# A nine-tap convolution moved from TensorE and VectorE to ScalarE products summed by accumulating transfers

## Chip, cores, metric

One core of one Trainium2 chip. The metric is the device time of one execution in microseconds (us). The kernel before takes 526.42 us, the median of three runs from 525.8 to 526.88 us.

## What is computed

Four sequences (chunks) of 512 tokens by 128 channels pass a gated convolution block and a mixture of 160 experts, each with a modulated layer norm and a residual. Cut to what matters:

```python
h = layernorm(x) * (1 + ca) + sa                 # modulation per chunk
h = rmsnorm(h) @ in_w.T + in_b                   # 128 -> 512
gate, val = sigmoid(h[..., :256]), h[..., 256:]
a = (dwconv4(val) @ A) @ Bm                      # four taps, rank 16
b = silu(dwconv9(val) + sym_b)                   # nine taps, per channel
y = concat([a @ ha.T, (b @ pw.T) @ hb.T]) @ fuse.T
x = x + ga * (h_attn_in + (gate * y) @ out_w.T + out_b)
h = layernorm(x) * (1 + cb) + sb
probs = sigmoid(h @ router_w.T)                  # top 8 of 160, normalized, times 2.5
x = x + gb * (sum_e combine_e * (silu(h @ w_gate_e.T) @ w_down_e.T) + shared(h))
```

`h_attn_in` is the modulated input, the block's own residual. The nine-tap branch is `b`: each channel of `val` is multiplied by nine weights at shifts of -4 to 4 tokens, and the products are added.

## The kernel before

Channels lie on the 128 partitions and the 512 tokens of a chunk along the free axis. The 256 channels of `val` are two halves, q = 0 and q = 1. Matmuls that need float32 accuracy are three float16 ones (`split`, L1159 to L1164: high by high, low by high, high by low).

**Experts.** Four experts make a duo; a chunk has 40 duos (`DUOS`), the kernel 160. For duo J, TensorE multiplies up (`up`, six matmuls), ScalarE applies silu out of PSUM (L803, two halves) and rounds the product with the combine weights to float16 (L822), VectorE multiplies by those weights (L1133, for the first two duos L1129 out of PSUM) and takes the rounding's rest (L1122), and TensorE multiplies down for duo J-4 (six matmuls, `LAG` = 4). SP loads the combine weights of a duo, broadcast, from a small HBM array (`c_all<-combine`), three duos ahead into a ring of four (`CRING`).

**Attention part.** It is cut into named items for a chunk. `walk` calls them in one written order, and every engine runs through that order for itself, doing its own share of each item: first the prologue (chunk 0 and part of chunk 1, setup, the first splits of the expert weights into high and low float16), then 160 times a duo followed by the items that the table `WITH` names for it. So an engine's queue is that order, filtered, and waits are on semaphores only. Items of chunk c+1 and c+2 are spread between the duos of chunk c.

**The nine taps before** come in two forms. For (chunk, half) in `BYDVE`, that is (0,1), (2,0), (2,1), (3,0), (3,1), TensorE makes `val` in a PSUM bank (`val0`, `val1`) and VectorE adds nine scaled shifts (`tapq:i`, L1030 and L1036). The bias part is an image `symb`, made by one matmul and copied by ScalarE (`setup(6)`, item `symb`). For (0,0), (1,0) and (1,1), TensorE does all: the input projection and each tap folded into one weight matrix (`wc_h`, `wc_l`), three matmuls for a tap, 27 for a half (`convq:i0:i1`), plus one for the bias. The folded weights of a half take a broadcast load, a multiplication (L866), a rounding (L630) and a subtraction (L870), for both halves.

**Residual.** `base0` (L1009) multiplies the modulated input by the output gain; `base1` adds it (L1012) and the gained bias (L1015) to `res` on VectorE; `x2` (L1064) adds the attention output. `ha` (L1002) adds the shift of the modulation, on VectorE.

**GpSimd** (POOL) does memsets, small copies and twelve tiny powers for norms (`rstd` L610, `rms` L613, `rstd2` L616). It issues no transfer.

**Order around the first duo.** The prologue holds chunk 0 whole, with its router (`max`, `swap`, `cw`, `sum`), the combine weights (`cT`, `c0`, `c1`), `conv` of chunk 1 up to tap 7, and seven splits of expert weights (`split_hi` on ScalarE L687, `split_lo` on VectorE L955); the other 13 follow in chunk 0's duos. Duo 0's product (L1129) needs `c0`; duo 2's needs the combine weights stored to HBM (`c_out`) and loaded again.

## Time and profile before

| | before |
|---|---|
| median of three runs | 526.42 us |
| profiled execution: span from first to last instruction | 523.2 us (the profile gives no other time for it; the median lies 3.2 us above) |
| TensorE busy | 510.4 us, 98% |
| VectorE busy | 492.7 us, 94% |
| ScalarE busy | 421.3 us, 81% |
| GpSimd busy | 27.6 us, 5% |
| mean granted TensorE clock | 0.997 |
| share of 16 transfer engines, the SP queue | 60.2% |

A busy time counts an instruction to its end, and the ends of one instruction and the start of the next overlap. How often an engine can start an instruction is read from the starts in the timeline. A shape such as 128x512 is partitions by elements.

### The profile page before, as it was taken

Reading aid. Unit: us, or ns where it says so; the run is one execution under the profiler, and the core shown is the slowest. Engines: PE = TensorE matmul, PEld = TensorE weight load, DVE = VectorE, ACT = ScalarE, POOL = GpSimd, SP = SyncE. Lnnn points to the kernel's source line nnn. Section 1 sums busy time; section 2 is a strip of 40 time slices with the busy share of each in tenths; the row PEclk is TensorE's granted clock in tenths of the full one; section 3 lists DMA queues with packets and bytes.
Section 4 is the critical chain, followed back from the end, with each engine's and each line's share of the span. In section 5 each row is a group of like instructions: output and inputs, shape, how many; then the busy total and the mean of one; then the engine's idle time right before and its main releaser. Section 6 shows DMA issues by size and latency. Waiting matters only on the chain.

```text
span 523.2 us, 7224 instructions
## 1 busy us (share of the span) xinstructions
PE 510.4 (98%) x2441; PEld 245.8 (47%) x2441; DVE 492.7 (94%) x630; ACT 421.3 (81%) x686; POOL 27.6 (5%) x45
## 2 busy tenths in 40 slices
PE   7989999999999999999999999999999999999996
PEld 5644544445454444444554444444553444444442
DVE  5999999999999999999999999999899799999995
ACT  5488899988999877787799877876799877777774
POOL 5100200004100000000100000000100000000000
PEclk9999999999999999999999999999999999999999
DMA  8897566645364666655455766665463676666650
GB/s 265 301 369 290 179 207 209 199 157 162 122 203 143 237 186 199 200 202 172 162 161 146 232 189 202 202 209 163 134 196 114 219 240 206 206 202 205 201 177 21
DMA packets 33309, 101.88 MB, mean 195 GB/s; under 512 B 3700, under 2 KB 8952, under 8 KB 33272
## 3 DMA queue, kind: packets, MB, share of 16 engines
q1 hardware_dynamic: 33272, 101.43, 60.2%
q8 instruction: 19, 0.31, 0.2%
q14 instruction: 18, 0.15, 0.1%
HBM read 98.52 MB, written 2.36 MB: 193 GB/s over the span
## 4 chain that ended last, share of the span: by engine, by line
PE 69%; DVE 19%; issue 5%; ACT 2%; DMA 2%; POOL 1%; SPq 1%; DVEq 0%; ACTq 0%
PE bank L1162 22%; PE bank L1164 21%; PE bank L1163 21%; DVE g_all L1122 7%; DVE s_all L1133 4%; DVE w L955 2%; PE bank L1309 2%; DMA res<-x_dram 2%; POOL rms L613 1%; PE bank L1319 1%; PE bank L1408 0%; DVE st L965 0%; DVE key L1099 0%; DVE s_all L1129 0%; ACT g_all L822 0%
## 5 line engine op out<-in xcount | busy, mean ns | idle before, releaser
L803 ACT ACTIVATE s_all<-bank 128x512 f32<-128x512 f32 x320 | 189.4, 594 | 69.4 <-PE bank L1164 68.5
L1122 DVE TENSOR_TENSOR g_all<-s_all,g_all 128x1024 f16<-128x1024 f32 x160 | 195.8, 1224 | 13.0 <-ACT g_all L822 12.7
L1133 DVE TENSOR_TENSOR s_all<-s_all,c_all 128x1024 f32<-128x1024 f32 x158 | 193.2, 1223 | 2.4 <-DMA c_all<-combine 2.4
L822 ACT ACTIVATE g_all<-s_all 128x1024 f16<-128x1024 f32 x160 | 168.2, 1052 | 2.1 <-DVE s_all L1133 1.9
L1162 PE MATMUL bank<-x_h,w 128*128 128x512 f16 x320 | 121.3, 379 | 1.0 <-ACT s_all L803 1.0
L1162 PE MATMUL bank<-g_all,w 128*128 128x512 f16 x320 | 121.3, 379 | 0.8 <-DVE g_all L1122 0.7
L1163 PE MATMUL bank<-g_all,w 128*128 128x512 f16 x320 | 121.3, 379 | 0.0
L1164 PE MATMUL bank<-g_all,w 128*128 128x512 f16 x320 | 121.3, 379 | 0.0
L1164 PE MATMUL bank<-x_l,w 128*128 128x512 f16 x320 | 121.3, 379 | 0.0
L1163 PE MATMUL bank<-x_h,w 128*128 128x512 f16 x320 | 121.3, 379 | 0.0
L1162 PEld LDWEIGHTS bank<-g_all,w 128*128 128x128 f16 x320 | 31.3, 98 | 41.0 <-DVE g_all L1122 3.6
L1162 PEld LDWEIGHTS bank<-x_h,w 128*128 128x128 f16 x320 | 31.3, 98 | 40.7 <-ACT s_all L803 4.6
L1163 PEld LDWEIGHTS bank<-g_all,w 128*128 128x128 f16 x320 | 31.3, 98 | 37.8 <-issue 1.3
L1164 PEld LDWEIGHTS bank<-g_all,w 128*128 128x128 f16 x320 | 31.3, 98 | 37.8
L1164 PEld LDWEIGHTS bank<-x_l,w 128*128 128x128 f16 x320 | 31.3, 98 | 37.8
L1163 PEld LDWEIGHTS bank<-x_h,w 128*128 128x128 f16 x320 | 31.3, 98 | 36.0 <-issue 1.3
L1036 DVE SCALAR_TENSOR_TENSOR attw<-bank,vec,attw 128x511 f32<-128x511 f32 (+3 forms) x40 | 29.9, 747 | 0.3
L955 DVE SCALAR_TENSOR_TENSOR w<-w 128x1024 f16<-128x1024 f32 x20 | 24.4, 1226 | 0.2 <-ACT w L687 0.2
L687 ACT ACTIVATE w<-w 128x1024 f16<-128x1024 f32 x20 | 20.8, 1054 | 0.6 <-DVE w L955 0.4
L613 POOL TENSOR_TENSOR rms<-mse,mhalf 128x4 f32<-128x4 f32 x4 | 9.5, 2378 | 197.8 <-DVE mse L977 197.8
L1309 PE MATMUL bank<-attw,wb 128*128 128x512 f32 x32 | 14.7, 592 | 0.0
L616 POOL TENSOR_TENSOR rstd<-ve,mhalf 128x4 f32<-128x4 f32 x4 | 6.7, 1685 | 136.2 <-DVE ve L1077 136.2
(236 smaller groups left out, 376.8 us busy)
## 6 DMA issues: line engine op xcount, KB each, us to landing
c_all<-combine SPq DMA_DIRECT2D x158, 512.0 KB, 4.5
w<-w_dram SPq DMA_DIRECT2D x20, 512.0 KB, 10.1
combine<-cT SPq DMA_DIRECT2D x4, 256.0 KB, 3.1
out_dram<-res SPq DMA_DIRECT2D x3, 256.0 KB, 3.0
s_all<-mats_dram SPq DMA_DIRECT2D x1, 640.0 KB, 6.7
attw<-symT_dram SPq DMA_DIRECT2D x1, 576.0 KB, 8.0
c_all<-symT_dram SPq DMA_DIRECT2D x1, 576.0 KB, 6.6
mod<-rows_mod SPq DMA_DIRECT2D x1, 576.0 KB, 4.4
```

The lines of the kernel that those rows point to most:

```text
L613: g.tensor_tensor(rms[:], mse[:], mhalf[:, 0:NT], ALU.pow).then_inc(s["rms_set"], 1)
L687: a(high(i), staged(i), ACT.Copy, scale=ES).then_inc(s["w_hi"], 1)
L803: a(sr[J % SRING][:, q * L:(q + 1) * L], U[q][:], ACT.Silu, scale=1.0 / ES).then_inc(s["s_done"], 1)
L822: a(gh[n % GRING], sr[n % SRING], ACT.Copy).then_inc(s["hi_set"], 1)
L955: e.scalar_tensor_tensor(out=low(i), in0=staged(i), scalar=ES, in1=high(i), op0=ALU.mult, op1=ALU.subtract).then_inc(s["w_lo"], 1)
L1036: e.scalar_tensor_tensor(out=acc[:, t0:t9], in0=val[:, t0 + d:t9 + d], scalar=v("sym_k", mid + d), in1=acc[:, t0:t9], op0=ALU.mult, op1=AL ...
L1122: e.tensor_tensor(gl[n % GRING], sr[n % SRING], gh[n % GRING], ALU.subtract).then_inc(s["lo_set"], 1)
L1133: e.tensor_tensor(sr[J % SRING], sr[J % SRING], cr[J % CRING], ALU.mult).then_inc(s["gm"], 1)
L1162: mm(dst, lh, rh, start=start, stop=False)
L1163: mm(dst, ll, rh, start=False, stop=False)
L1164: return mm(dst, lh, rl, start=False, stop=stop)
L1309: last = mm((A1, A2)[q][:], wb[:, i, q * P:(q + 1) * P], s32[:, i, :], start=False, stop=(i == ML - 1))
```

## The change

- `BYACT`: the nine taps of chunks 1, 2 and 3, both halves, are now items `mulq:i`. ScalarE computes tap i as `scale * val + bias` from the PSUM bank, `scale` the tap's weight and `bias` that weight times the projection's bias; the middle tap goes straight to the accumulator `s32`, the other eight alternately to one of two buffers for a half (`part`). GpSimd issues for each of the eight a transfer that adds the buffer to `s32` in SBUF; it waits for the product and for the transfer before on that half. ScalarE waits before tap i > 2 until the transfer of tap i-2 has landed, as it reuses that buffer.
- (0,0) stays with TensorE, (0,1) with VectorE. The folded weights exist for half 0 only, and `symb` for half 1 of chunk 0 only: a broadcast load, L866, L630, L870 and the image for the other half go.
- `base1` of chunks 1 to 3 is two adding transfers from GpSimd, `ha` of chunks 2 and 3 one each.
- The order is new throughout. Items `ss`, `cT`, `c0`, `c1`, `cT_sb` of chunk 0 come after duo 0 instead of before it; three more splits come after it.

```diff
-BYDVE = ((0, 1), (2, 0), (2, 1), (3, 0), (3, 1))
+BYPE = ((0, 0),)
+BYDVE = ((0, 1),)
+BYACT = ((1, 0), (1, 1), (2, 0), (2, 1), (3, 0), (3, 1))
...
-        18: ((2, "ha"),),
-        19: ((1, "ya0"), (11, "split_lo"), (12, "split_hi"),),
...
+        18: ((1, "mul0:8"), (11, "split_lo"), (1, "gate"),),
+        19: ((1, "mul1:8"),),
...
+        4: ((3, "nb"), (2, "mul1:2"), (2, "zl"), (2, "base0"), (2, "mul0:3"), (2, "mul0:4"), (2, "zh"),
+            (2, "mul1:3"),),
+        5: ((2, "gate"),),
+        6: ((2, "mul1:4"), (3, "t1b"),),
...
+        15: ((3, "ha"), (2, "mul0:7"),),
+        16: ((2, "mul1:7"),),
+        18: ((2, "zmv"), (2, "mul0:8"), (2, "mul1:8"), (2, "base1"),),
+        20: ((2, "tanh0"), (3, "rms"), (3, "square"),),
+        21: ((2, "wo"),),
+        22: ((2, "silu0"),),
...
+def shifts(i):
+
+    d = (0, 1, -1, 2, -2, 3, -3, 4, -4)[i]
+    return d, max(0, -d), L - max(0, d)
...
-        wc_h, wc_l = sb("wc_h", [P, KS * DI], F16), sb("wc_l", [P, KS * DI], F16)
+        pbuf = sb("pbuf", [P, 2 * L + KS * P])
+        kb = sb("kb", [P, ML * KS])
...
+        def part(q, i):
+
+            at = (1 - q) * 2 * L + i % 2 * L
+            return pbuf[:, at:at + L]
...
-            sp.dma_start(pool_d[:, 2048:2048 + KS * P], symT[:, KS * P:].broadcast_to([P, KS * P])).then_inc(s["ld_sym1"], 16)
...
+                elif n[0:3] == "mul" and n[5] != "0":
+                    q, i = int(n[3]), int(n[5])
+                    d, t0, t9 = shifts(i)
+                    turns = rounds(c, q)
+                    pool.wait_ge(s[f"mul{q}"], turns * KS + i + 1)
+                    if i > 1:
+                        pool.wait_ge(s[f"add{q}"], 16 * (turns * (KS - 1) + i - 1))
+                    g.dma_start(s32[:, q, t0:t9], part(q, i)[:, t0:t9], accum_op=ALU.add).then_inc(s[f"add{q}"], 16)
+                elif n == "ha" and c > 1:
+                    pool.wait_ge(s["h_set"], c + 1)
+                    g.dma_start(h[:], modr(c, 0), accum_op=ALU.add).then_inc(s["ha_dma"], 16)
+                elif n == "base1" and c:
+                    tiles = slice(c * NT, c * NT + NT)
+                    pool.wait_ge(s["u_set"], c + 1)
+                    g.dma_start(res[:, tiles, :], t1[:], accum_op=ALU.add).then_inc(s["base_dma"], 16)
+                    pool.wait_ge(s["base_dma"], 32 * c - 16)
+                    pool.wait_ge(s["gob_set"], c + 1)
+                    g.dma_start(res[:, tiles, :], over(gob[:], NT), accum_op=ALU.add).then_inc(s["base_dma"], 16)
...
+                elif n[0:3] == "mul":
+                    q, i = int(n[3]), int(n[5])
+                    d, t0, t9 = shifts(i)
+                    done = rounds(c, q) * (KS - 1)
+                    if i == 0:
+                        act.wait_ge(s["val_ps"], vals(c, q) + 1)
+                        act.wait_ge(s["kb_set"], 2)
+                        act.wait_ge(s["y_ps"], 2 * c)
+                        if q == 0:
+                            act.wait_ge(s["conv_ps"], len(BYPE))
+                    elif i > 2:
+                        act.wait_ge(s[f"add{q}"], 16 * (done + i - 2))
+                    mid = q * KS + PADL
+                    a((part(q, i) if i else s32[:, q, :])[:, t0:t9], (A1, A2)[q][:, t0 + d:t9 + d], ACT.Identity,
+                      bias=kb[:, mid + d:mid + d + 1], scale=v("sym_k", mid + d)).then_inc(s[f"mul{q}"], 1)
...
-                   dynamic_dma_scratch_size=1024)
+                   dynamic_dma_scratch_size=2048)
```

How the order moves work, at three places. First VectorE from the router's last step of chunk 0 (`cw<-cw,rs`) to duo 2; `w<-w` is a split of expert weights, `s_all<-s_all,bank` the product of duo 0 or 1, `g_all<-s_all,g_all` the rest for duo 0. Before:

```order
L1116 TENSOR_TENSOR cw<-cw,rs 128x640
L965 BN_STATS st<-res 128x6 x4
L969 BN_AGGR mv<-st 128x2 x4
L972 TENSOR_SCALAR ve<-mv 128x4
...
L955 SCALAR_TENSOR_TENSOR w<-w 128x1024
L1009 TENSOR_TENSOR t<-h,mod 128x512
L955 SCALAR_TENSOR_TENSOR w<-w 128x1024 x2
L1129 TENSOR_TENSOR s_all<-s_all,bank 128x512 x2
L1012 TENSOR_TENSOR res<-t,res 128x512
L1015 TENSOR_TENSOR res<-gob,res 128x512
L1129 TENSOR_TENSOR s_all<-s_all,bank 128x512 x2
L1122 TENSOR_TENSOR g_all<-s_all,g_all 128x1024
```

The change:

```order
L1180 TENSOR_TENSOR cw<-cw,rs 128x640
L1028 BN_STATS st<-res 128x6 x4
L1032 BN_AGGR mv<-st 128x2 x4
L1035 TENSOR_SCALAR ve<-mv 128x4
L1193 TENSOR_TENSOR s_all<-s_all,bank 128x512 x2
L1018 SCALAR_TENSOR_TENSOR w<-w 128x1024
L1074 TENSOR_TENSOR t<-h,mod 128x512
L1108 SCALAR_TENSOR_TENSOR wo<-outT,mod 128x256
L1112 TENSOR_TENSOR gob<-brow,mod 128x128
L1018 SCALAR_TENSOR_TENSOR w<-w 128x1024
L1193 TENSOR_TENSOR s_all<-s_all,bank 128x512 x2
L1044 SCALAR_TENSOR_TENSOR nb<-mv,rstd 128x4
```

Before, two statistics (the second, the same three rows, is left out above), three splits and `t<-h,mod` stand between the router and duo 0's product; now one statistic does, and the splits come after the product.

Second, ScalarE in the change from the table load of the prologue to duo 0's silu. `pbuf<-bank,kb,vec` and `attw<-bank,kb,vec` are the new products of chunk 1, all of which stand here without a counterpart before:

```order
L819 ACTIVATE dum<-vec 128x1
L736 ACTIVATE w<-w 128x1024
L800 ACTIVATE attw<-bank,kb,vec 128x512
L800 ACTIVATE pbuf<-bank,kb,vec 128x511
L767 ACTIVATE zp<-bank,zb 128x512
L800 ACTIVATE attw<-bank,kb,vec 128x512
L800 ACTIVATE pbuf<-bank,kb,vec 128x511
L816 ACTIVATE h<-res,nb,rstd 128x128 x4
L800 ACTIVATE pbuf<-bank,kb,vec 128x511
L830 ACTIVATE x<-bank,sbc,cbc 128x512
L831 ACTIVATE x_h<-bank,sbc,cbc 128x512
L800 ACTIVATE pbuf<-bank,kb,vec 128x511
```

Six of the 54 products come in the prologue, twelve of chunk 1 and two of chunk 2 in chunk 0's duos.

Third, GpSimd's queue in the change, for chunk 2 (before, it holds only the powers): the small power operations stand in one line with the transfers.

```order
L651 DMA attw<-pbuf 128x509 x3
L654 DMA h<-mod 128x4x128
L651 DMA attw<-pbuf 128x508 x4
L658 DMA res<-t 128x512
L661 DMA res<-gob 128x4x128
L664 TENSOR_TENSOR rms<-mse,mhalf 128x4
L667 TENSOR_TENSOR rstd<-ve,mhalf 128x4
```

## Rows read from the trace of the kernel before

**Rows 1.** The page: busy time of each engine.
```profile
PE 510.4 (98%) x2441; PEld 245.8 (47%) x2441; DVE 492.7 (94%) x630; ACT 421.3 (81%) x686; POOL 27.6 (5%) x45
```

**Rows 2.** Windows, one for each chunk's duos: PE, PEld, DVE, ACT, POOL busy, clock, DMA.
```profile
56.16:172.43 116.27, 116.08 (x553) 54.10 (x550) 115.79 (x135) 108.03 (x174) 9.03 (x3) 1.00 0.56 176
172.43:289.93 117.50, 117.50 (x565) 56.11 (x564) 116.49 (x141) 95.93 (x157) 2.92 (x2) 1.00 0.58 185
289.93:407.61 117.68, 116.72 (x557) 55.25 (x556) 113.86 (x134) 92.98 (x144) 1.91 (x1) 1.00 0.58 182
407.61:523.20 115.59, 111.47 (x515) 50.13 (x513) 98.89 (x86) 85.53 (x127) 0.00 (x0) 1.00 0.60 190
```

**Rows 3.** TensorE's timeline (start us, us): first matmul of duos 130 and 135.
```profile
435.06 0.38 PE L1162 MATMUL bank<-x_h,w 128*128 128x512 f16 x1
...
448.01 0.38 PE L1162 MATMUL bank<-x_h,w 128*128 128x512 f16 x1
```

**Rows 4.** VectorE's timeline: duo 0's product, duo 40's product.
```profile
58.75 1.28 DVE L1129 TENSOR_TENSOR s_all<-s_all,bank 128x512 f32<-128x512 f32 x2
...
177.00 1.23 DVE L1133 TENSOR_TENSOR s_all<-s_all,c_all 128x1024 f32<-128x1024 f32 x1
```

**Rows 5.** TensorE's timeline: first conv of chunk 1, first matmul of duo 0.
```profile
40.35 0.39 PE L1162 MATMUL bank<-hnT,wc_h 128*128 128x512 f16 x1 [2.47 <-DVE hnT L1019]
...
56.16 0.38 PE L1162 MATMUL bank<-x_h,w 128*128 128x512 f16 x1
```

**Rows 6.** VectorE's timeline: router's last step, then three splits and more.
```profile
51.22 0.83 DVE L1116 TENSOR_TENSOR cw<-cw,rs 128x640 f32<-128x640 f32 x1
...
54.74 1.22 DVE L955 SCALAR_TENSOR_TENSOR w<-w 128x1024 f16<-128x1024 f32 x1
55.88 0.69 DVE L1009 TENSOR_TENSOR t<-h,mod 128x512 f32<-128x512 f32 x1
56.48 2.35 DVE L955 SCALAR_TENSOR_TENSOR w<-w 128x1024 f16<-128x1024 f32 x2
```

**Rows 7.** ScalarE's timeline: combine weights spread, `c0`; then copied, `cT_sb`.
```profile
52.07 0.63 ACT L784 ACTIVATE h<-cw 128x512 f32<-128x512 f32 x1 [1.18 <-DVE cw L1116]
...
53.23 0.60 ACT L796 ACTIVATE cT<-bank 128x512 f32<-128x512 f32 x1
```

**Rows 8.** DMA issues: KB each, median us to landing.
```profile
c_all<-combine SPq DMA_DIRECT2D x158, 512.0 KB, 4.5
...
combine<-cT SPq DMA_DIRECT2D x4, 256.0 KB, 3.1
```

**Rows 9.** VectorE's timeline: one of the 45 taps, and what follows it.
```profile
22.02 0.74 DVE L1036 SCALAR_TENSOR_TENSOR attw<-bank,vec,attw 128x511 f32<-128x511 f32 x1
22.68 0.15 DVE L981 SCALAR_TENSOR_TENSOR nb<-mv,rstd 128x4 f32<-128x4 f32 x1
```

**Rows 10.** ScalarE's timeline: bank to SBUF with scale and bias; split, silu, rounding.
```profile
44.52 0.77 ACT L766 ACTIVATE x_h<-bank,sbc,cbc 128x512 f16<-128x512 f32 x1
45.18 1.05 ACT L687 ACTIVATE w<-w 128x1024 f16<-128x1024 f32 x1
...
98.12 1.06 ACT L687 ACTIVATE w<-w 128x1024 f16<-128x1024 f32 x1
99.07 0.60 ACT L803 ACTIVATE s_all<-bank 128x512 f32<-128x512 f32 x1
99.55 1.06 ACT L822 ACTIVATE g_all<-s_all 128x1024 f16<-128x1024 f32 x1
```

**Rows 11.** Costliest groups: GpSimd's power; its timeline; VectorE's in that stretch.
```profile
L613 POOL TENSOR_TENSOR rms<-mse,mhalf 128x4 f32<-128x4 f32 x4 | 9.5, 2378 | 197.8 <-DVE mse L977 197.8
...
119.17 6.45 POOL L613 TENSOR_TENSOR rms<-mse,mhalf 128x4 f32<-128x4 f32 x1 [62.34 <-DVE mse L977]
...
123.51 1.24 DVE L1133 TENSOR_TENSOR s_all<-s_all,c_all 128x1024 f32<-128x1024 f32 x1
124.65 0.70 DVE L1059 SCALAR_TENSOR_TENSOR attw<-attw,bank 128x512 f32<-128x512 f32 x1
```

More of the change, by code:

```diff
@@ L127 @@
-    {
-        1: ((2, "ss"), (3, "tap0:4"),),
-        2: ((3, "tap0:5"), (3, "wo"), (3, "tap0:6"),),
-        4: ((3, "tap0:7"),),
-        6: ((3, "tap0:8"),),
-        8: ((3, "tap1:0"), (3, "z"),),
-        10: ((3, "tap1:1"), (3, "zh"),),
-        14: ((3, "zl"),),
-        15: ((3, "tap1:2"),),
-        17: ((3, "silu0"), (3, "tap1:3"),),
-        18: ((3, "tap1:4"), (3, "base0"), (3, "zmv"),),
-        19: ((3, "gate"),),
[10 rows of a table removed]
-        34: ((3, "logit"), (3, "prob"), (3, "max"), (3, "swap"), (3, "cw"),),
-        35: ((3, "sum"),),
+        0: ((4, "split_lo"), (0, "ss"), (0, "cT"), (1, "base0"), (0, "c0"), (0, "cT_sb"), (1, "mul1:3"), (1, "wo"),
+            (5, "split_lo"),),
@@ new lines @@
+    {
+        1: ((3, "mul0:2"),),
+        4: ((3, "mul0:3"), (3, "mul1:2"), (3, "wo"),),
+        7: ((3, "mul1:3"),),
+        8: ((3, "mul1:4"), (3, "mul0:4"),),
+        10: ((3, "mul1:5"),),
+        11: ((3, "mul0:5"),),
+        12: ((3, "zh"), (3, "zl"),),
+        14: ((3, "mul0:6"), (3, "mul1:6"),),
+        15: ((3, "zmv"),),
+        17: ((3, "mul0:7"), (3, "mul1:7"), (3, "gate"), (3, "tanh0"), (3, "mul0:8"),),
+        20: ((3, "mul1:8"),),
+        23: ((3, "silu0"), (3, "silu1"),),
+        24: ((3, "ya0"), (3, "yb0"), (3, "gy0"), (3, "gy1"), (3, "ya1"), (3, "tanh1"), (3, "yb1"),),
+        26: ((3, "o0"), (3, "o1"), (3, "x2"), (3, "bn"),),
+        27: ((3, "nb2"),),
+        29: ((3, "t2a"),),
+        30: ((3, "t2b"),),
+        31: ((3, "xh"), (3, "turn2"), (3, "base1"), (3, "xl"),),
+        34: ((3, "prob"), (3, "logit"), (3, "max"), (3, "swap"), (3, "cw"), (3, "sum"),),
+        35: ((3, "shup"),),
@@ L151, with before, vals, rounds @@
         36: ((3, "c_out"),),
         37: ((3, "norm"),),
-        39: ((3, "cT"), (3, "shup"), (3, "cT_sb"), (3, "ss"),),
+        38: ((3, "cT_sb"), (3, "ss"), (3, "cT"),),
     },
-    {},
-)
-def by_dve(c, q):
-    return sum(b < (c, q) for b in BYDVE)
+    {
+        27: ((3, "rstd2"),),
+    },
+)
+def before(table, c, q):
+    return sum(b < (c, q) for b in table)
+def vals(c, q):
+    return before(BYDVE, c, q) + before(BYACT, c, q)
+def rounds(c, q):
+    return sum(b[1] == q and b[0] < c for b in BYACT)
@@ L214, in walk @@
-    att(0, "conv0:8:9")
-    att(0, "base0")
-    att(0, "gate")
     att(0, "tap1:5")
@@ L219, in walk @@
     setup(7)
+    att(1, "t1a")
     att(0, "tap1:7")
     att(0, "tap1:8")
-    att(1, "t1a")
+    att(1, "t1b")
+    setup(3)
+    att(0, "conv0:2:4")
+    setup(8)
     att(0, "silu0")
+    att(0, "silu1")
+    att(0, "tanh0")
+    att(1, "hm")
+    att(0, "conv0:4:5")
+    att(1, "ha")
+    split_lo(0)
+    att(1, "rms")
+    att(0, "tanh1")
+    split_lo(1)
+    att(0, "conv0:5:7")
+    att(0, "conv0:7:8")
+    att(0, "conv0:8:9")
+    att(0, "gate")
+    att(1, "square")
+    split_hi(2)
@@ L243, in walk @@
+    att(0, "table")
+    split_hi(3)
     att(0, "base1")
[L244 to L256 removed]
+    att(1, "mul0:0")
+    att(1, "mul0:1")
+    att(1, "zh")
+    att(0, "x2")
+    att(1, "mul1:0")
+    att(0, "bn")
+    att(0, "o1")
+    att(1, "zl")
     att(0, "nb2")
[L258 removed]
+    att(1, "mul1:1")
@@ L295, in walk @@
-    att(1, "conv1:6:7")
-    att(0, "ss")
-    att(0, "cT")
-    att(3, "stat")
-    split_lo(4)
-    att(1, "conv0:7:8")
-    att(0, "c0")
-    att(0, "cT_sb")
-    att(0, "c1")
-    att(1, "base0")
-    split_lo(5)
-    split_hi(6)
-    split_lo(6)
+    att(0, "cw")
+    att(0, "logit")
+    att(0, "sum")
+    att(1, "base1")
+    att(3, "stat")
+    att(0, "shup")
     for c in range(B):
```

415 lines of the change are left out of this document (192 added, 223 removed), and 10 rows, old and new, of the table WITH.

## The prediction

> **What bounds the kernel now.** Busy shares first [rows 1]: TensorE 98%, VectorE 94%, ScalarE 81%. That does not decide between the first two, and busy time counts overlapping ends, so I go to starts in the timeline. Duos 130 and 135, where little else runs, begin 12.95 us apart [rows 3]: 60 matmuls, 0.216 us each, 2.59 us a duo. VectorE starts a 1024-wide operation every 1.14 us [rows 11], so its two cost 2.28 us a duo. ScalarE starts the next operation 0.48 us after a silu and 0.95 us after a 1024-wide one [rows 10], so 0.48 + 0.95 + 0.48 = 1.91 us a duo. Per duo TensorE is longest; what counts is what the attention items add. The windows by chunk [rows 2] show TensorE busy 116.08 of 116.27, 117.50 of 117.50, 116.72 of 117.68 and 111.47 of 115.59 us, at clock 1.00. From duo 0 at 56.16 us [rows 5] on, TensorE hardly pauses. But in chunk 0's duos VectorE is as full (115.79 of 116.27); its products of duos 0 and 40 lie 118.25 us apart [rows 4].
>
> So work taken from TensorE pays at once, and work taken from VectorE only where VectorE is as long, in chunk 0's duos. In the prologue what counts is when duo 0 can start.
>
> **TensorE.** Removed: 54 matmuls of the two convs of chunk 1, their two bias matmuls and one `symb` matmul; added: six for `val` of chunk 1. Net 51 x 0.216 = 11.0 us. Of these, 45 - 6 = 39 (8.4 us) stood before duo 0; the other 12 (2.6 us) after it. The transposes of `cT`, `c0` and `c1` move behind duo 0: 24 of 0.11 us, 2.6 us. After duo 0's first matmul TensorE thus has what it had: no gain there. The whole gain of 11.0 us lies before duo 0, if something else does not hold duo 0 up.
>
> **What holds duo 0 up.** Without the convs TensorE in the prologue waits for the router's chain, not the reverse. Before, the router's last step starts at 51.22 and duo 0's product at 58.75 [rows 4, 6]: 7.5 us, in which VectorE does that step, two statistics, three splits (3 x 1.14) and `t` (0.6). In the change one statistic stays; but the product needs `c0`, that is two spreads on ScalarE (1.16 us from the first to `cT` [rows 7]) and transposes (0.9 us). The product then starts 0.8 + 2.1 = 2.9 us after the last step starts, 4.6 us sooner. The router's chain itself: earlier in the prologue a broadcast multiplication and a subtraction for half 1 leave VectorE, its copy leaves ScalarE, and `hnT` of chunk 0 no longer queues behind three small copies; much of this was hidden by the matmuls of the first conv, which stay. Against it, four products of chunk 1 (4 x 0.66 [rows 10]) now stand ahead of the layer norm's operations on ScalarE. I take 1 us sooner, between -1 and +2.5. Together duo 0's product comes 5.6 us sooner, at about 53.1.
>
> A second gate is duo 2: combine weights must be copied, stored (3.1 us) and loaded (4.5 us [rows 8]). With the last step at 50.2 this gives 50.2 + 0.8 + 1.2 + 1.2 (copies) + 7.6 = 61 us. VectorE gets to duo 2's product at 53.1 + 1.2 + 3.5 (two splits, `t`, `wo`, `gob`) + 1.2 + 1.2 + 1.1 = 61.3. So it costs nothing, with no margin.
>
> **Chunk 0's duos.** VectorE sheds three taps of 0.66 us [rows 9], `ha`, the two adds of chunk 1's `base1` and chunk 2's `base0`: 4.5 us. It takes three splits, chunk 1's `base0` and `wo`: 4.6 us. It keeps 118.3 us. ScalarE takes 14 products x 0.66 = 9.3 us, `ss`, the spreads and `cT_sb` (3.9 us) and one split more (0.95), and loses `symb` and one `zh`: about +12.5 us. Adding its instructions by their starting intervals gives 101.8 us before, so 114.3 now. TensorE has 114 to 115 us. All three engines lie between 114 and 118.3: VectorE sets the stage, and ScalarE is in its queue nearly without slack. From duo 0's product at 53.1 VectorE would be at duo 40 at 171.4 instead of 177.0. I allow 1 us for ScalarE being late for its two partners: 4.6 us gained.
>
> **Chunks 1 and 2.** VectorE sheds 15 + 4, then 14 taps, and the residual adds: some 13 and 11 us. It was not the longest there, so this is worth nothing except the pauses behind it, at most 1 us (117.68 - 116.72 [rows 2]). ScalarE takes 20 x 0.66 = 13.2 and 14 x 0.66 = 9.2 us: busy 95.9 and 93.0 of some 117.5 us [rows 2], so it fits. `z` of chunk 2 (three matmuls, 0.65 us) crosses into chunk 1's duos: +0.65 us. Chunk 3's duos and the end stay.
>
> **The adding transfers.** 48 of 256 KB, plus 6 for `base1` and 2 for `ha`. No row shows one. The nearest are a plain 256 KB store, 3.1 us, and the 512 KB load, 4.5 us [rows 8]; their bounds here are 3 and, if GpSimd is as slow at issuing as at its slowest power, 6.45 + 3.1 = 9.5 us [rows 11]. I take 4.5, nearest to the loads they run beside. The shortest cover is in chunk 1's duos: `mul1:2` after duo 4, `mul1:4` after duo 6 waits for its transfer, 5.2 us later. Elsewhere it is four duos or more, though before `silu0` two transfers in a row must fit in 22 - 18 = 4 duos. So at 4.5 us nothing waits. Traffic grows by 14 MB, from 56 to 58% of the engines to some 65% [rows 2], and loads run three duos (7.8 us) ahead at 4.5 us. A late product blocks ScalarE, and behind it stand the silus for which TensorE waits with only two banks: every us of such a wait is lost in full.
>
> Here a rule speaks against the change. In rows 11 GpSimd's power on 128x4 lasts 6.45 us while VectorE runs 1024-wide operations with both inputs in SBUF, and ends when one comes whose second input is a bank; the other three of its line take (9.5 - 6.45) / 3 = 1.0 us each. The Trainium skill (SBUF — State Buffer, Who interferes with whom) says that a VectorE operation with two SBUF inputs blocks GpSimd's reads, while writing descriptors is stopped by VectorE's two-port modes only, and infers that `tensor_tensor` leaves it alone. The trace agrees on the reads; on descriptors no run here shows it. By that rule the issues stay short and my sum stands. For the transfer itself its page DMA: Bandwidth & Descriptors (Anatomy of one DMA) gives about 2.0 us + bytes / 436 GB/s, which would be 2.6 us and change nothing in the sum.
>
> **Sum.** 4.6 us gained to duo 40, 0.65 us lost, some 0.5 us of pauses gained: 4.5 us. The profiled span 523.2 becomes 518.7, and the median, 3.2 us above that span, 526.4 - 4.5 = 521.9 us.
>
> **Rivals.**
> - *Slow transfers (slower).* If issue to landing takes L over 5.2 us, ScalarE waits L - 5.2 at `mul1:4`, and from some 5.5 us on also at the silus (two in a row against four duos), about 1.5 x (L - 5.2) more. For three chunks: 7.5 x (L - 5.2). The 4.5 us of gain are gone at L = 5.8; at L = 7.5 it is 17 - 4.5 = 12.5 us slower, 539 us. For it: 6.45 us [rows 11], a busy VectorE, 56 issues. Against: the other three powers of that line take 1.0 us, and VectorE has gaps in chunks 1 and 2 now. A milder form, two or three places, ends at 527 to 533. Chance 0.19 in all.
> - *ScalarE sets chunk 0's duos.* Before, it stood still 116.3 - 101.8 = 14.5 us there, not being the bound. If only half of that goes away, the stage lasts 114.3 + 7 = 121.5 instead of 118.3 and takes 3 to 4 us of the gain: 525 to 526.5 us. For: three full engines in one chain. Against: rings of four duos. Chance 0.15.
> - *The prologue gives all.* If the router's chain moves up too and TensorE is full from duo 0, up to 11.0 us go: 516 to 518 us. Against: 7.6 us of store and load before duo 2, and VectorE's 118.3 us. Chance 0.08.
> - *The forecast*, 518.5 to 524.5 us: 0.58.
>
> **Numbers.** 521.9 us. The range from 517.5 to 529.5 takes in the forecast, ScalarE's case, most of the gain case and the mild part of the slow transfers. A measurement tells this kernel from no change at about 0.2% (1.05 us). Faster by more: 0.58 + 0.08 and a little of ScalarE's case, 0.68. Within: 0.09. Slower: 0.23.
>
> **What would show it.** Right: duo 0's matmuls near 47 us, its product near 53, duo 40's near 171 to 172; TensorE idle between duo 0 and duo 2 and then full; products of 0.66 us spacing; transfers landing in 4 to 5 us; VectorE's idle time grown to 10 us and more in chunks 1 and 2; ScalarE about 455 us busy. Wrong: ScalarE idle ahead of a product or a silu, released by a transfer; a transfer over 5.2 us; chunk 0's duos over 120 us; a later router.

## The result, and the profile after the change

The change makes the kernel slower: 541.14 us in the median of four runs (535.01 to 546.59), against 526.65 us before (525.8 to 526.97), a ratio of 1.0256 with a 95% interval from 1.0221 to 1.0291. The forecast was 521.9 us, with 529.5 us as the upper end. The profiled execution is the shortest of the four: 535.01 us, of which 533.2 us are the span. That the runs lie 11 us apart, where those of the kernel before lie 1.2 us apart, is part of what has to be explained; the comparison itself leaves disturbed runs out.

From the page of the changed kernel: busy shares, the two DMA queues, and the chain that ended last.

```profile
PE 505.3 (95%) x2390; PEld 243.4 (46%) x2390; DVE 465.8 (87%) x585; ACT 450.1 (84%) x738; POOL 76.1 (14%) x103
...
q1 hardware_dynamic: 33128, 100.84, 57.1%
q0 software_dynamic: 9984, 14.62, 16.7%
...
PE 60%; DMA 25%; ACT 5%; issue 4%; DVE 3%; POOL 2%; SPq 1%; POOLq 0%; ACTq 0%; DVEq 0%
```

The work moved as planned: TensorE has 51 matmuls fewer than in [rows 1], which is 11.0 us at 0.216 us each, and VectorE is far from full. TensorE's busy time fell by only 5.1 us, though: its matmuls take longer at a lower clock (mean granted clock in the first 56 us 0.88, before 0.97), and ahead of each pause the last one counts with its whole 0.38 us and not with the 0.216 us to the next start. But a quarter of the chain that ended last is DMA, and the queue of the adding transfers (q0) takes 16.7% of the engines' time for 14.62 MB, twice as much per byte as q1. Next the windows by chunk, from the first matmul of duos 5, 40, 80 and 120 to the next of them (PE, PEld, DVE, ACT, POOL busy, granted clock, DMA share, GB/s). They answer to [rows 2], except that the first starts at duo 5.

```profile
69.55:175.07 105.52, 103.77 (x498) 49.09 (x497) 103.34 (x117) 102.42 (x167) 18.34 (x18) 1.00 0.75 214
175.07:301.46 126.39, 120.72 (x571) 56.00 (x569) 105.02 (x121) 108.80 (x181) 19.75 (x22) 1.00 0.79 217
301.46:417.85 116.39, 116.08 (x555) 54.92 (x554) 102.38 (x114) 101.13 (x159) 17.09 (x18) 1.00 0.80 221
417.85:533.20 115.35, 111.21 (x515) 50.35 (x513) 100.35 (x87) 85.51 (x127) 0.00 (x0) 1.00 0.58 187
```

Before, duo 5 began at 66.81 us, and the same stretches took 105.62, 117.50, 117.68 and 115.59 us. The 10.0 us that the span grew are thus 2.7 ahead of duo 5, 8.9 in chunk 1's duos, and 1.6 gained back elsewhere. The DMA issues of the changed kernel (KB each, median us to landing) beside [rows 8]:

```profile
c_all<-combine SPq DMA_DIRECT2D x158, 512.0 KB, 4.8
...
attw<-pbuf POOLq DMA_DIRECT2D x12, 255.5 KB, 5.9
...
attw<-pbuf POOLq DMA_DIRECT2D x12, 254.0 KB, 7.1
...
res<-t POOLq DMA_DIRECT2D x3, 256.0 KB, 6.5
```

The four groups of them (12 each) have medians of 5.9, 6.2, 6.4 and 7.1 us, all 48 together 6.4 us, where 4.5 was forecast. GpSimd's waits (us in total, times, longest) and its timeline at the end of chunk 2's branch show what that does in one queue:

```profile
POOL attw L651 <- DMA attw<-pbuf: 115.2, 24, 7.6
...
POOL res L661 <- DMA res<-t: 19.5, 3, 9.2
```

```profile
239.08 1.23 POOL L658 DMA_DIRECT2D res<-t  x1
249.56 1.30 POOL L661 DMA_DIRECT2D res<-gob  x1 [9.25 <-DMA res<-t]
250.34 1.58 POOL L664 TENSOR_TENSOR rms<-mse,mhalf 128x4 f32<-128x4 f32 x1
```

GpSimd issues one transfer for each half of `s32`, then has to wait until the first has landed before it may issue the next into the same half. Everything behind it waits too: here chunk 3's `rms` stands 9.25 us behind a residual transfer. ScalarE then waits in its own queue, ahead of silus that TensorE needs:

```profile
224.60 0.77 ACT L800 ACTIVATE pbuf<-bank,kb,vec 128x508 f32<-128x508 f32 x1 [1.92 <-DMA attw<-pbuf]
...
231.80 0.77 ACT L800 ACTIVATE pbuf<-bank,kb,vec 128x508 f32<-128x508 f32 x1 [1.92 <-DMA attw<-pbuf]
...
244.09 0.63 ACT L783 ACTIVATE attw<-attw 128x512 f32<-128x512 f32 x1 [2.11 <-DMA attw<-pbuf]
...
251.95 1.28 ACT L759 ACTIVATE hr<-h,rms 128x128 f32<-128x128 f32 x4 [2.17 <-POOL rms L664]
```

These four waits add up to 8.1 us, against 8.9 us that chunk 1's duos grew. The kernel without product transfers (below) takes 118.97 us for these duos, with 570 matmuls for 565: 1.5 of the 8.9 us are not the transfers', 7.4 are.

### The profile page after: what moved, and what is told of

Read it like the earlier page. It is cut to its first block, busy times and chain, and to the rows that moved or that the text cites. A ratio compares the mean times of both kernels' runs of the same rounds, so it can differ in the third digit from the quotient of the medians.

```text
span 533.2 us, 7225 instructions
## 1 busy us (share of the span) xinstructions
PE 505.3 (95%) x2390; PEld 243.4 (46%) x2390; DVE 465.8 (87%) x585; ACT 450.1 (84%) x738; POOL 76.1 (14%) x103
## 3 DMA queue, kind: packets, MB, share of 16 engines
q0 software_dynamic: 9984, 14.62, 16.7%
## 4 chain that ended last, share of the span: by engine, by line
PE 60%; DMA 25%; ACT 5%; issue 4%; DVE 3%; POOL 2%; SPq 1%; POOLq 0%; ACTq 0%; DVEq 0%
DMA attw<-pbuf 19%; PE bank L1226 18%; PE bank L1228 18%; PE bank L1227 18%; DMA res<-t 3%; PE bank L1366 2%; DMA idf<-idf_dram 1%; ACT s_all L868 1%; PE bank L1376 1%; ACT g_all L887 1%; DMA mod<-rows_mod 1%; POOL attw L651 1%; PE bank L1310 1%; POOL rms L664 1%; PE bank L1237 1%
## 5 line engine op out<-in xcount | busy, mean ns | idle before, releaser
L887 ACT ACTIVATE g_all<-s_all 128x1024 f16<-128x1024 f32 x160 | 170.3, 1065 | 1.0 <-DVE s_all L1197 1.0
L651 POOL DMA_DIRECT2D attw<-pbuf x48 | 43.0, 976 | 200.8 <-DMA attw<-pbuf 115.2
L1226 PEld LDWEIGHTS bank<-x_h,w 128*128 128x128 f16 x320 | 31.3, 98 | 47.2 <-ACT s_all L868 13.6
L800 ACT ACTIVATE pbuf<-bank,kb,vec 128x511 f32<-128x511 f32 (+3 forms) x48 | 37.5, 796 | 3.9 <-DMA attw<-pbuf 3.8
```

Source lines behind the costliest of these rows:

```text
L651: g.dma_start(s32[:, q, t0:t9], part(q, i)[:, t0:t9], accum_op=ALU.add).then_inc(s[f"add{q}"], 16)
L800: a((part(q, i) if i else s32[:, q, :])[:, t0:t9], (A1, A2)[q][:, t0 + d:t9 + d], ACT.Identity, bias=kb[:, mid + d:mid + d + 1], scale=v(" ...
L887: a(gh[n % GRING], sr[n % SRING], ACT.Copy).then_inc(s["hi_set"], 1)
L1226: mm(dst, lh, rh, start=start, stop=False)
```

## Experiments on the transfers

Edits are against the changed kernel. The experiments ran in five groups, and those of a group share their runs of the kernel before, whose medians were 524.29, 525.37, 525.89, 525.27 and 525.51 us.

**Small transfers.** Most of the sum is left out.

```
- g.dma_start(s32[:, q, t0:t9], part(q, i)[:, t0:t9], accum_op=ALU.add)
+ g.dma_start(s32[:, q, t0:t0 + 32], part(q, i)[:, t0:t0 + 32], accum_op=ALU.add)
```

> Every adding transfer of a product moves 32 columns of the 512 and the rest of the sum is left out; the issues, the waits and their order are unchanged. Theory A (the transfers are slow because of their bytes: the 16 DMA engines are 0.96 to 1.04 busy in every stretch in which adding transfers run, and each transfer takes 6.4 us in the median): they land in 2.5 to 3.5 us, the stretch of chunk 1's duos falls from 126.4 us to 117 to 119, and the kernel from about 541 to 527 to 532 us. Theory B (the fixed cost of an adding transfer and GpSimd's one queue, in which each issue waits for the transfer two before it): they still take over 5 us, the stretch stays above 124 us and the kernel above 537 us.

```profile
attw<-pbuf POOLq DMA_DIRECT2D x48, 16.0 KB, 3.5
```

A transfer of 16 KB lands in 3.5 us, so 2.9 of the 6.4 us go with the bytes. The transfer engines are full while the adding transfers run: windows of the kernel before, the changed one and this one (columns as in [rows 2], the last two figures the DMA share and GB/s):

```profile
180.00:200.00 20.00, 20.00 (x94) 9.33 (x93) 19.96 (x21) 15.26 (x24) 0.00 (x0) 1.00 0.67 202
...
180.00:200.00 20.00, 20.00 (x94) 9.33 (x93) 16.78 (x18) 19.10 (x31) 3.52 (x5) 1.00 0.98 279
...
180.00:200.00 20.00, 20.00 (x94) 9.35 (x93) 16.85 (x17) 19.12 (x31) 5.40 (x7) 1.00 0.69 199
```

In the profiled execution (527.15 us) chunk 1's duos take 118.97 us and no product waits for a transfer: theory A. But the other three runs took 535.15 to 536.99 us, so something else, not seen in that profile, costs 8 us at times.

**Residual adds by VectorE.** `base1` and `ha` of chunks 1 to 3 become `tensor_tensor` operations again, `base1` behind `gob` in `wo`.

> The residual adds and the shift's add of chunks 2 and 3 go back to VectorE (some 1.1 us each); the transfers of the products stay. Theory C (it is the residual transfers, which stand in GpSimd's queue ahead of rms and of products): the stretch of chunk 1's duos falls from 126.4 us to 119 or less. Theory A (the products' transfers): only the gap before chunk 3's rms goes, 2 to 3 us, so 123 to 124.5 us, and the kernel gains 2 to 4 us. VectorE has the room: 105 us busy of 126.

533.6 us (531.14 to 535.52). Chunk 1's duos take 123.95 us, 2.4 less: theory A's number, not theory C's. The residual transfers are the smaller part.

**Half the work.** `BYDVE = ((0, 1), (2, 1), (3, 1))`, `BYACT = ((1, 0), (1, 1), (2, 0), (3, 0))`; items named `mul` of the moved halves run as taps.

> Half 1 of chunks 2 and 3 goes to VectorE's fused steps (9 of 0.66 us each, 6 us more in each of the stretches of chunks 1 and 2, where VectorE is busy 105 of 126 and 102 of 116 us); half 0 and chunk 1 stay with the products and transfers. Theories A and B both: the queue is half empty, ScalarE no longer waits for transfers in chunk 1's duos, the stretch falls from 126.4 us to 117 to 119 and the kernel by 8 to 9 us. If the stretch stays above 123 us, the loss there isn't the transfers but something else that the change moved (VectorE's load, the items' order).

537.84 us (536.29 to 540.55), a miss in the total. Chunk 1's duos do fall to 119.61 us, but duos 5 to 40 take 114.84 us in place of 105.52, with one pause of TensorE of 8.0 us from 83 us on. Its cause stood in GpSimd's timeline: chunk 3's `rstd`, a power of four numbers per partition, took 13.64 us from 71.71 to 85.35.

**Chunk 3's statistics earlier.** `att(3, "stat")` moves from behind `att(1, "base1")` to ahead of `att(0, "max")`.

> The statistics of chunk 3 come ahead of the router's maxima, so that on GpSimd its rstd stands ahead of chunk 1's residual transfers and runs near 57 us, before the stretch in which VectorE has no pause. In the profile of the run before last that rstd took 13.64 us from 71.71 (four numbers per partition; 1.6 to 2.3 us in the other profiles), ended when VectorE came to a stop, kept chunk 1's next transfers from being issued, and TensorE stood still for 8.1 us. Theory S (this is what makes some runs 5 to 13 us longer than the profiled one, not the transfers themselves): rstd takes 1 to 2 us, all the runs come to lie within 2 us of each other, and the median falls from about 541 to 532 to 535 us. Rival (the spread has another cause, such as the clock or the transfers): the runs still spread over 5 us or more.

539.16 us (535.35 to 544.17). `rstd` runs at 55.94 us in 1.76 us, as meant, but the runs still lie 9 us apart. The rival holds for this run: `rstd` is one cause of the scatter, not the only one. Its profile (544.17 us) has four pauses of TensorE of 0.88 to 4.15 us between 97 and 361 us, the longest in chunk 2's duos, where a product waits 4.62 us for a transfer.

**The changed kernel again.**

> The changed kernel once more, for more times and a second profile. By theory S, rstd of chunk 3 takes over 6 us near 70 us in a profile that is 5 us or more longer than 535, and TensorE then stands still for 3 to 8 us near duo 10; by the rival the extra time lies in many small stalls of the later duos. Times between 535 and 547 us.

551.34 us (543.19 to 555.13), above the expected span of times. The profile (554.72 us) has both: `rstd` for 13.57 us, and longer stalls later (127.41 us for chunk 1's duos, 123.37 for chunk 2's). Around `rstd`, by engine, from the four timelines:

```profile
73.41 13.57 POOL L643 TENSOR_TENSOR rstd<-ve,mhalf 128x4 f32<-128x4 f32 x1
86.95 0.92 POOL L651 DMA_DIRECT2D attw<-pbuf  x1
...
84.87 1.22 DVE L1197 TENSOR_TENSOR s_all<-s_all,c_all 128x1024 f32<-128x1024 f32 x1
93.62 1.23 DVE L1186 TENSOR_TENSOR g_all<-s_all,g_all 128x1024 f16<-128x1024 f32 x1 [7.54 <-ACT g_all L887]
...
91.39 0.78 ACT L800 ACTIVATE pbuf<-bank,kb,vec 128x509 f32<-128x509 f32 x1 [9.23 <-DMA attw<-pbuf]
...
92.70 0.61 PE L1226 MATMUL bank<-x_h,w 128*128 128x512 f16 x1 [8.23 <-ACT s_all L868]
```

Read in order: GpSimd's power does not end while VectorE runs eleven operations in a row on two inputs in SBUF. VectorE stops at 84.87 + 1.22 = 86.09, only because ScalarE has come to the product whose transfer stands behind the power in GpSimd's queue; the power ends at 86.98, and the transfer is issued. So the queue behind a GpSimd operation is what stops the engine that keeps GpSimd from ending. In all five profiles with a long power there it ends 0.9 us after the last operation before VectorE stops. Of nine profiles in which this `rstd` stands behind chunk 1's residual transfer, near 70 us, five show it at 8.1 to 15.2 us and four at 1.6 to 2.3; in the other eight profiles it comes before 60 us and never took over 2.2 us. With the power at 13.6 to 15.2 us duos 5 to 40 take 114.0 to 115.4 us, at 8.1 us 111.2, and 104.3 to 107.0 in the others but one (112.3, the first repaired version below). In the short cases VectorE's operations on two inputs run without a visible pause too (in the changed kernel one from 69.33 and the next from 70.47, the power from 69.80 to 71.44), so a full VectorE stands beside every long power and does not by itself bring one. The Trainium skill (SBUF — State Buffer, Who interferes with whom) states that a VectorE operation with two SBUF inputs contends with a GpSimd instruction that reads SBUF, and that issue order decides who blocks. The trace agrees on the first with 13.57 us; of the second it shows that a single power that waits gets no turn between operations of VectorE that all started after it. It also infers that writing descriptors is not held up by `tensor_tensor`; the trace agrees, the issues of `attw<-pbuf` take 0.86 to 1.23 us in both profiles of the changed kernel, but for one of 1.65 us in each.

The windows of the same profile show what follows (granted clock in the third column from the right, 1.00 for 2.4 GHz, 0.50 for 1.2):

```profile
80.00:85.00 5.00, 4.48 (x21) 1.86 (x19) 5.00 (x6) 2.15 (x4) 5.00 (x1) 1.00 0.74 236
85.00:87.50 2.50, 0.00 (x0) 0.00 (x0) 1.09 (x1) 0.00 (x0) 2.50 (x2) 1.00 0.39 151
87.50:92.50 5.00, 0.00 (x0) 0.00 (x0) 0.00 (x0) 1.11 (x2) 0.91 (x2) 0.53 0.54 151
92.50:97.50 5.00, 4.80 (x12) 1.77 (x13) 2.89 (x3) 4.92 (x9) 2.08 (x3) 0.50 0.79 120
97.50:100.00 2.50, 2.50 (x12) 1.06 (x11) 1.83 (x2) 1.16 (x2) 0.71 (x1) 0.89 0.83 204
```

After the 8.2 us without a matmul TensorE's clock is at its lower level, and it stays there for 5 us of matmuls. Duos 5 to 40 take 115.37 us, 9.9 more than in the first profile.

**No transfer of products**, and then **no adding transfer at all**. The sum is left out but for the centre tap; the silus wait for the products alone. The second also has the residual adds by VectorE.

> The 48 transfers of products are left out, and with them the sum (each chunk keeps only its centre tap); the 54 products and the 8 residual transfers stay. What is missing from the time is then what these transfers cost in all. Theory T (they make nearly all of the loss behind the prologue, by stalls and by the clock that falls after each stall): chunk 0's duos 105.5 us, chunk 1's 117 to 118, the kernel at 524 to 528 us. Rival (the loss lies in the prologue and in ScalarE's extra work): above 532 us.

> As the run before, and the residual adds and shift adds by VectorE, so that no adding transfer is left. Theory T: the runs lie within 1.5 us of each other, as the kernel before does, and the median is the one of the run before or 1 us less; duo 5 still starts at 69 to 72 us, so the prologue's lateness is not the transfers'. Rival (the spread of the runs comes from the prologue's clock): the runs spread over 4 us or more without a transfer.

528.03 us (526.66 to 528.99) and 529.27 us (528.88 to 529.89); ratios to before 1.0039 (1.0024 to 1.0054) and 1.0053 (1.0035 to 1.0072). Windows of the first of the two:

```profile
69.40:173.67 104.27, 103.82 (x498) 49.16 (x497) 102.95 (x117) 102.14 (x167) 13.74 (x5) 1.00 0.61 187
173.67:292.64 118.97, 118.97 (x570) 56.54 (x569) 104.94 (x121) 108.36 (x181) 6.63 (x6) 1.00 0.66 197
292.64:409.03 116.39, 116.08 (x554) 54.97 (x553) 102.37 (x114) 101.13 (x159) 3.24 (x2) 1.00 0.60 184
```

Theory T holds: the 48 transfers cost 541.14 - 528.03 = 13 us of the changed kernel's median, and with them the scatter goes. How much they cost depends on the set of runs: by the ratios to the kernel before it is 11 us (1.0256 against 1.0039) for the changed kernel's first set and 17 us (1.0365) for its second, which ran in this group. ScalarE's 54 products cost nothing here: chunk 1's duos are full of matmuls (118.97 us, 570 of them, where [rows 2] has 565 in 117.50). The median with the residual adds on VectorE is 1.2 us above that with them as transfers: as far as two medians show it, that part of the change, alone, was worth about that much. In the second one GpSimd's `rms` takes 7.59 us at 133.76, without one adding transfer in the kernel, and ends 0.9 us after VectorE starts an operation with an input in PSUM (140.41): the long powers do not come from the transfers.

**48 transfers with nothing between them**: chunk 3's statistics early and the residual adds on VectorE.

> All 48 transfers of products stay; only chunk 3's statistics come early and the residual and shift adds go to VectorE. If what hurts is the long residual transfers and an rstd in GpSimd's queue, the time falls to 529 to 532 us and the runs lie within 1.5 us, as in the attempt with 32 transfers. If it is the number of transfers, the stalls in chunk 1's duos stay (stretch over 122 us) and the time is 532 us or more.

537.8 us (537.32 to 538.64). The scatter is gone: it comes from what stands between the product transfers (an `rstd`, residual transfers). The stalls are not: 121.82 and 119.29 us for chunks 1 and 2. The transfers themselves cost without scatter too: 537.8 against 529.27 us with none, 8.5 us. Not all of that is stalls, as the order of the prologue differs by the statistics: of the 7.6 us between the two profiled spans 5.8 lie behind duo 5 and 1.8 ahead of it, where the transposes of the combine weights ran at a lower clock in this profile (router's last step to duo 0's product 4.67 us, in the other 3.02).

## Experiments on the prologue

**Matmuls with no use** to keep the clock up: 14 behind chunk 1's `z`, 6 behind chunk 0's second transposes.

> 20 matmuls with no use (16-bit, 128x512, into a bank that is free) keep TensorE busy before the first duo: 14 behind chunk 1's z projection, 6 behind chunk 0's second transposes. Theory P (TensorE's granted clock of 0.62 to 0.69 in 45:55 makes the chain to the router late): the clock stays at 1.00 there, the logits take 1.0 us in place of 2.1, duo 5 starts 1.5 to 2.5 us sooner than at 69.55, and the kernel gains as much. Theory Q (the lateness is ScalarE's and the order's, not the clock's): duo 5 stays within 0.5 us of 69.55 or comes later.

534.79 us (533.09 to 540.68). The clock is 1.00 from 40 to 55 us, and from the logits to the router's last step it takes 4.90 us in place of 5.92. But duo 5 starts at 70.88. The gain of 1.0 us was lost ahead of it, as in this run the clock was at its lower level from 10 to 18 us and the output projection at 39.45: the router's last step starts at 55.64, in the changed kernel at 55.74. And behind it the clock fell again: it is 0.50 in 57.5:60, and duo 0's product comes 4.48 us after the router's last step in place of 3.02. The same shows when the changed kernel's two profiles are put side by side (first the one of 535.01 us, then the one of 554.72 us), in the transposes that the product waits for:

```profile
57.18 0.60 PE L1418 MATMUL bank<-idf,cw 128*128 128x128 f32 x4
57.62 0.60 PE L1430 MATMUL bank<-idf,h 128*128 128x128 f32 x4
...
58.01 1.06 PE L1418 MATMUL bank<-idf,cw 128*128 128x128 f32 x4
58.86 1.06 PE L1430 MATMUL bank<-idf,h 128*128 128x128 f32 x4
```

From the router's last step to the product it takes 3.02 us in the first and 4.66 in the second; the profiles of this case lie between 3.0 and 4.7. So the clock is worth 1.0 us ahead of the router's last step and up to 1.6 behind it. It does not explain the 4.5 us by which that step came late.

**Two places on TensorE**: the first warming matmuls behind the fold, `turn` of chunk 1 behind `o0`.

> Two steps of the prologue change places on TensorE: the warming matmuls that wait for idf (2.06 us at 10.80) go behind the fold matmuls, and chunk 1's first transposes go behind chunk 0's output projection. Theory Q1 (the prologue is late because of these places): the output projection starts at 35.4 to 37.0 us in place of 38.27, duo 5 at 66.8 to 68.0 in place of 69.55, and the kernel gains 1.5 to 2.5 us. Theory Q2 (ScalarE is what sets the first duos, so that an earlier TensorE finds it busy all the same): duo 5 stays within 0.7 us of 69.55.

547.02 us (540.01 to 553.15), with `rstd` at 14.27 us. The output projection is at 39.20, no sooner: Q1 missed. Duo 5 starts at 71.84, 2.3 us later, so Q2 missed too. But the row of the fold tells why it comes no sooner, and a later run tests it: TensorE waits for GpSimd.

```profile
12.40 1.19 PE L1251 MATMUL bank<-c_all,s_all 128*128 128x128 f32 x4 [4.20 <-POOL c_all L632]
```

**Two products later**, `mul1:3` and `mul1:4` of chunk 1 from duos 0 and 1 to 3 and 4.

> Two products of chunk 1 (0.66 us each) go from the items of duos 0 and 1 to those of duos 3 and 4; nothing else changes. Theory Q2 (from 55.3 us on ScalarE has no pause and sets the first duos): duo 5 starts 0.7 to 1.3 us sooner than at 69.55. Theory Q1 (TensorE's own order and clock): it stays within 0.4 us.

543.74 us (537.25 to 545.28), duo 5 at 71.39. From duo 0's product (60.88) to duo 5 it takes 10.5 us, where the changed kernel takes 10.8 (58.76 to 69.55): 0.3 us less, where the two products are 1.3 us. For Q2 that is a miss in size, and no more than a hint. (Duo 0's product itself came 2.1 us later in this run, 1.6 of it in the transposes ahead of it.)

**GpSimd's tables first**, and the warming matmuls that wait for `idf` behind the fold, as before the change:

```
-    att(0, "stat")
     setup(0)
+    att(0, "stat")
     setup(1)
     setup(20)
-    setup(30)
...
     setup(2)
+    setup(30)
```

> Undoes one step of the new order at the start: GpSimd copies the first tables for the fold ahead of chunk 0's rstd again, as the kernel before did, and the warming matmuls that wait for idf go behind the fold. In the run with the order of idf alone, TensorE waited 4.20 us for GpSimd's last table at 12.40; before, the fold began at 9.37. Theory G (the prologue's first loss is GpSimd's queue, in which the tables stand behind a wait for chunk 0's statistics): the fold begins at 9.3 to 10 us, the first taps at 18.7 to 19.5 in place of 21.08, and the output projection 1 to 2 us sooner than at 38.27. Theory P (the clock): the first taps stay later than 20.5. The time stays scattered between 533 and 550 us, since the transfers are unchanged.

```profile
9.12 0.71 PE L1251 MATMUL bank<-c_all,s_all 128*128 128x128 f32 x4 [0.94 <-DMA s_all<-mats_dram]
```

Theory G holds, for the two places together. The change had put chunk 0's statistics ahead of `setup(0)`, and GpSimd, which waits for VectorE there, came to the first of its some 20 table operations 3.6 us later (6.42 in place of 2.81 us) and to the last 2.4 us later (10.7 in place of 8.3); no row ahead of the prediction shows GpSimd's start. In the changed kernel the warming matmuls stood ahead of the fold as well: they waited for `idf` until 10.80, and the fold started at 11.80 right behind them, when GpSimd's last table (from 10.71) was done. With these matmuls moved alone the fold waited for GpSimd until 12.40; the tables alone were not tried, and an estimate from these rows is that they would have left the fold at 11.80. Both undone, the fold starts at 9.12 in place of 11.80, the first taps at 18.23 in place of 21.08, the output projection at 36.02 in place of 38.27, duo 5 at 68.56 in place of 69.55. The time is 542.59 us (540.75 to 545.44), for `rstd` takes 15.17 us in its profile.

## Repaired versions

**All repairs but one**: the order on TensorE, statistics early, two products later, 32 transfers.

> All the repairs together: the order of the prologue, chunk 3's statistics earlier, two products of chunk 1 later, and half 1 of chunks 2 and 3 by VectorE, so that 32 transfers are left of 48. From the rows: duo 5 at 67 to 68 (before: 66.81), 105.5 us to duo 40, 117.5 to 119.5 us for chunk 1's duos, 116.4 and 115.4 for the last two: 522 to 525 us of span, so 524 to 527 us, about as long as the kernel before, with all runs within 2 us. If the transfers were bad in themselves, by the DMA engines that they fill, the kernel would stay above 530 us.

533.43 us (533.07 to 538.13). Above the expectation: the profile, of the longest run, has duo 5 at 72.62 and two pauses of TensorE near 126 and 130 us (2.98 and 1.40 us), where chunk 1's silus wait 3.27 and 1.60 us for transfers; the granted clock is then 0.60 in 132.5:135.

**The same with the residual adds on VectorE**, and TensorE's order left.

> The attempt at a version that keeps the change's idea with the least in GpSimd's queue: 32 transfers, all residual adds on VectorE, chunk 3's statistics early, two products later. By theory T the stalls in chunk 0's duos stay (chunk 1 still has its 16 transfers), 529 to 533 us; to beat the kernel before it would need under 523 us.

530.54 us (530.01 to 530.96), as expected. Duos 5 to 40 take 105.53 us, which was not: the 16 transfers of chunk 1 stall little once nothing else stands in GpSimd's queue: ScalarE waits 1.6 us for transfers in all.

**And the prologue in the places of before**: tables first, gate products and `base1` ahead of a split and of `low` on VectorE, `o0` ahead of `turn`, 16 matmuls with no use, `wo` of chunk 1 later.

> The attempt with 32 transfers, plus a prologue in the places of the kernel before: the tables first, VectorE's gate products and residual adds ahead of a weight split and of chunk 1's low half, the output projection ahead of chunk 1's transposes, 16 matmuls with no use to keep TensorE busy ahead of the logits, chunk 1's output weights later. From the milestones: output projection at 35 to 36 us, router's last step at 51 to 52.5 in place of 56.0, duo 5 at 66.5 to 68 in place of 71.3, and so 525.5 to 527.5 us, a tie with the kernel before. If duo 5 stays above 70 us, ScalarE's and VectorE's work in the first duos sets it and not the chain to the router.

527.66 us (526.69 to 528.85), ratio 1.0043 (1.0023 to 1.0062). Router's last step at 52.22, duo 5 at 67.21, both as expected: of the 4.5 us by which the chain was late, 3.5 were orders and the clock, and can be undone. But it is still not faster than before.

**Chunk 1's branch left out** of that version.

> The repaired version, with chunk 1's nine-tap branch left out altogether: no product of chunk 1 on ScalarE (18 of 0.66 us, 7 of them ahead of duo 5) and no transfer (16). It shows what was to be had by taking the branch off TensorE if its new place cost nothing. Theory Q2 (ScalarE's products and the transfers give back what TensorE was spared): duo 5 starts 2.5 to 4 us sooner than at 67.21, duos 5 to 40 take 104.3 us in place of 106.75, and the time is 521 to 523 us, below the kernel before at last. If instead duo 5 stays within 1 us of 67.21, the start is bound by something that both kernels share, and the branch's place was never the question.

525.49 us (523.3 to 526.34), ratio 0.9994 (0.9978 to 1.0010). Duo 5 starts at 63.42, 3.8 us sooner, as Q2 says, but duos 5 to 40 take 106.19 us, not 104.3, chunk 1's 120.04, and the total misses its 521 to 523. No more was to be had in this version by a branch of chunk 1 at no cost at all: a tie. None of the versions beats the kernel before.

First matmuls of duos 5, 40, 80 and 120 in TensorE's timeline give the stretches of the profiled executions:

| kernel | duo 5 at | duos 5 to 40 | chunk 1's | chunk 2's | chunk 3's, end | span |
|---|---|---|---|---|---|---|
| before | 66.81 | 105.62 | 117.50 | 117.68 | 115.59 | 523.2 |
| changed | 69.55 | 105.52 | 126.39 | 116.39 | 115.35 | 533.2 |
| changed, again | 71.36 | 115.37 | 127.41 | 123.37 | 115.39 | 552.9 |
| no product transfers | 69.40 | 104.27 | 118.97 | 116.39 | 115.37 | 524.4 |
| 48, nothing between | 73.54 | 105.66 | 121.82 | 119.29 | 115.39 | 535.7 |
| 32, residuals on VectorE | 71.32 | 105.53 | 120.42 | 116.39 | 115.34 | 529.0 |
| that, prologue repaired | 67.21 | 106.75 | 120.04 | 116.39 | 115.41 | 525.8 |

## Why the prediction was wrong

- *TensorE sheds 11.0 us, all ahead of duo 0.* Right in count, 51 matmuls, but busy time fell from 510.4 to 505.3 us only, 5.1. What was freed ahead of duo 0 became idle time and slower matmuls: duo 0's matmuls start at 53.13 in place of 56.16, and then wait for the combine weights.
- *The router's chain 1 us sooner.* This step failed: the last step starts at 55.74, not 50.2, 4.5 us later than in [rows 6]. I had counted what left VectorE and ScalarE and not what the new order put ahead of what on GpSimd and VectorE. By milestones against before: first taps 2.0 us later (GpSimd's tables and the matmuls that wait for `idf`), 1.9 us more up to `x2`, 0.4 us gained back until the logits, and 1.0 us more from there to the last step by the clock (granted clock 0.62 in 45:50 and 0.69 in 50:55; 5.92 us, against 4.92 before at 1.00 and 4.90 in the kernel with useless matmuls): together 4.5. The tables and the `idf` matmuls were tested together, the clock alone (with matmuls of no use); VectorE's order only together with the rest, so that the 1.9 us are not shown to be its.
- *2.9 us from the router's last step to duo 0's product.* Right in this profile, 3.02 us, and with luck: it holds only while TensorE's clock stays up, and was 4.66 us in the second profile of the same kernel. The two rows of VectorE, timeline:

```profile
55.74 0.82 DVE L1180 TENSOR_TENSOR cw<-cw,rs 128x640 f32<-128x640 f32 x1
...
58.76 1.28 DVE L1193 TENSOR_TENSOR s_all<-s_all,bank 128x512 f32<-128x512 f32 x2 [0.80 <-PE bank L1430]
```

  So duo 0's product, forecast 5.6 us sooner, comes at 58.76, where it was (58.75). From there to duo 2's product it takes 8.16 us, as forecast (8.2), and before 4.85: two splits, `t`, `wo` and `gob` now stand between them. That is why duo 5 starts 2.7 us later although the product is not late.
- *Chunk 0's duos 118.3 us by VectorE, 1 us allowed.* Near: products of duos 0 and 40 lie 120.36 us apart (58.76 and 179.12). In the kernel without product transfers it is 119.11, within the 1 us allowed; the other 1.25 us are the transfers' (one silu of chunk 1 waits 2.00 us for one). ScalarE as the bound of this stage did not come.
- *Chunks 1 and 2.* VectorE's relief was worth 1.3 us in chunk 2's duos, 1 forecast.
- *A transfer lands in 4.5 us, so nothing waits.* This step failed and cost most. They take 6.4 us; the 512 KB load beside which I had put them was no measure for an accumulating transfer inside SBUF. The rival with slow transfers had the right mechanism and side; its formula gives 7.5 x (6.4 - 5.2) = 9.0 us of stalls over three chunks, and against the kernel without product transfers the profile has 1.3 in chunk 0's duos, 7.4 in chunk 1's and none in chunk 2's, 8.7 together. That the two sums agree is in part luck: the formula spreads them evenly and begins at `mul1:4`, while the waits came at the last products, the silus and `rms`. With both steps put right the forecast's own sum comes out: 518.7 + 5.6 + 9.0 = 533.3 us, and the profiled span is 533.2. What the rival left out is that GpSimd's power may take 13.6 us with transfers behind it; this made other runs longer still. The row was there: 6.45 us in [rows 11], which I had used as a bound for an issue and not for what stands behind it in the queue.
- *Range.* 529.5 was set from the mild form of that rival. The profiled execution misses it by 5.5 us, the median by 11.6.

Not settled: what decides, from run to run, whether the power ends beside a full VectorE (1.64 us) or only once VectorE stops (13.57 us), and why chunk 2's transfers stall some executions by 3 to 5 us near duo 99 and others not at all.

## What to carry to other kernels

A transfer that computes is priced from its own row, not from a plain one, and then by its queue: with one queue and two buffers, two transfers per landing time is all there is, and everything else in that queue (a residual add, an `rstd`) waits and makes others wait. Before putting anything behind a GpSimd operation that reads SBUF, look at how full VectorE is in that stretch; in the long cases here the wait ended when VectorE stopped. Where a change reorders a prologue, follow the moved waits on every engine's queue, the least busy one too: some 20 small operations on GpSimd and a few matmuls that wait for a load moved the start of all the rest.
